# Attention stream of a six-block kernel: the output steps one to two steps later, the next layernorm two steps later

## The chip, the cores and the metric

One core of one Trainium2 chip. The time is the device time of the program in microseconds; less is better.

## What is computed

x is [4, 256, 256] (1024 tokens of 256). Six blocks are added to it in turn: a mixture of experts block (ffn0), an attention without softmax (attn0), ffn0 again, a second mixture of experts (ffn1), a softmax attention (attn1), and ffn1 again. The change lies in attn1 and in what attn1 prepares for the last ffn1:

```
h = layernorm(x)
c_kv = h @ w_dkv.T;  q = (h @ w_q.T), 16 heads of 16
k = c_kv @ w_uk.T;   v = c_kv @ w_uv.T
scores = q k^T / 4 + alibi (slope 0.0625, causal), softmax
x = x + (attn v) @ w_o.T
x = x + 0.5 * ffn1(layernorm(x))
```

With 4 sequences of 256 tokens and 16 heads there are 64 pairs of sequence and head, called heads 0 to 63 here.

## The kernel before

Each engine runs its own list of instructions, written out by hand, and waits on counting semaphores. In attn1 all five lists share one step counter s, from 0 to 77 (64 heads and SUM = 14 steps to drain). What an engine does at a step, in this order:

- TensorE (attn1, from line 1126): scores(s) for s under 64 (lines 1231 and 1234; an even head has two matmuls, an odd one one); scores_t(s-7), the scores once more in transposed form with the softmax shift in them (L1263, L1265); at s mod 4 = 1 shift_turn, four transposes of the shifts of four heads (L1246); at s = 14, 18, ... 74 pv of the next group of four heads, 16 small matmuls (L1282); then the output steps; then project_v at V_STEPS; then at Z_STEP the eight transposes of the next layernorm's result (L808).
- VectorE (from line 2263): bias_min(s), which adds the bias and takes the row minimum (L2319; three parts for an even head, one for an odd); at s mod 4 = 3 shift_hi and shift_lo (L2335, L2340); then its output steps; then at LN_STEPS[0] the layernorm statistics of the first half of x (L1768, L1774).
- ScalarE (from line 1638): out_hi; at s mod 4 = 1 shift_out (L1681); probs(s-7), the exponential (L1688); at LN_STEPS[1] normalise (L1387, four instructions); at s mod 4 = 3 out_t, which copies the result of pv to SBUF (L1695); v_out one step after project_v (L1635); z_hi one step after Z_STEP (L1394, two instructions).
- GpSimd: mask(hd) for each head (L711), and before mask(LN_STEPS[0] - TURN + 1) the scale of the layernorm (ln_scale, L650 to L660).
- SyncE: the DMAs that load the stacks of q and k. They have no step of the list.

**The output steps.** The result of a sequence n (0 to 3), tile t (0 or 1) comes from pv transposed. It is turned back (out_back, TensorE, L1297, four transposes), divided by the softmax sum (out_norm, VectorE, L2348 and L2350), turned again (out_turn, TensorE, L1304, two transposes), split in a rounded part (out_hi, ScalarE, L1699) and a remainder (out_lo, VectorE, L2356), projected with w_o (out_project, TensorE, L793 to L795, six matmuls), and added to x (out_add, VectorE, L2364). OUT_STEPS are TensorE's steps of (back, turn, project) for t = 0 and then for t = 1, counted from 16 n, for n = 0 to 2. VectorE and ScalarE do their part at the step after the one that they follow. n = 3 is done after the loop, in the list of the last ffn1, from out_back on.

All output steps of a sequence, and project_v for n = 2 and 3, use PSUM bank 7. So they wait for each other:

```
def out_back(n, t):                      # TensorE, L1288
    pe.wait_ge(ot_s, 4 * (n + 1))        # out_t of the four groups
    if t == 0 and n < 2:
        pe.wait_ge(v_s, 3 + n)           # v_out
    ...
    elif 2 * n + t:
        pe.wait_ge(yt_s, 2 * n + t)      # the out_add before
```

project_v(3) waits for yt_s of out_add (0,1); out_turn waits for out_norm, out_project for out_hi and out_lo. scores_t(hd) waits for probs(hd-2), and scores of an odd head hd for bias_min(hd-2), of an even head for bias_min(hd-4). The statistics of the next layernorm wait for out_add (1,1); its transposes wait for normalise and for all 64 bias_min; z_hi waits for them. SyncE's list, the weights and all shapes are the same in both kernels.

Of the kernel before, what the change touches and what calls it, by code (L numbers as in the profile page):

```python
# [61 lines left out]
GROUP = 4  # L62
TURN = 7
SUM = 14
OUT_STEPS = (28, 30, 33, 35, 37, 39)
V_STEPS = (25, 41)
LN_STEPS = (57, 61)
Z_STEP = 66
HALF = PAIRS // 2
SLOTS = 16  # L70
STACKED = 16 * 9
# [10 lines left out]
def program(nc, x_in, w0, w1, wr, pre, posts, att0, r0, ident_in, cap_in, iota_in, wa, rows_in, bias_in, split_out, z_rows, y_rows,  # L82
            out,
            stages=STAGES):
    with ExitStack() as ctx:
# [540 lines left out]
        def _(pool):  # L626
# [11 lines left out]
            def ln_scale(p):  # L638
                if p >= norms:
                    return  # L640
                kind = stages[NORMS[p][0]]

                if kind == "ffn0":
                    mul, add = 1.0 + RMS_EPS, RMS_EPS * LN_EPS
                else:
                    mul, add = 1.0, LN_EPS
                pool.wait_ge(mv_s, p + 1)
                if p:
                    pool.wait_ge(zs_s, p)
                nc.gpsimd.tensor_scalar(zs_e[:, :], mv[:, :, 1], mul, add, ALU.mult, ALU.add).then_inc(zse_s, 1)  # L650
                pool.wait_ge(zse_s, p + 1)
                if p:
                    pool.wait_ge(z_s, p)
                if p >= BY_ACT:
                    nc.gpsimd.tensor_scalar(mean_n[:, :], mv[:, :, 0], -1.0, None, ALU.mult).then_inc(mean_n_s, 1)
                nc.gpsimd.tensor_tensor(zs[:, :], zs_e[:, :], half[:, :], ALU.pow).then_inc(zs_s, 1)
                if p >= BY_ACT:
                    pool.wait_ge(mean_n_s, p - BY_ACT + 1)
                    pool.wait_ge(zs_s, p + 1)
                    nc.gpsimd.tensor_tensor(shift_z[:, :], mean_n[:, :], zs[:, :], ALU.mult).then_inc(shift_z_s, 1)  # L660
# [92 lines left out]
            for st in plan:  # L753
                for b in range(2):
# [19 lines left out]
                    elif b == 0:  # L774
                        ln_scale(st.p + 1)
                        for hd in range(4 * HEADS):
                            if hd == LN_STEPS[0] - TURN + 1:
                                ln_scale(st.p + 2)
# [12 lines left out]
        def _(pe):  # L791
# [334 lines left out]
            def attn1(st):  # L1126
# [16 lines left out]
                for s in range(4 * HEADS + SUM):  # L1143
# [15 lines left out]
                    for n in range(3):  # L1159
                        if s - HEADS * n in OUT_STEPS:  # L1160
                            i = OUT_STEPS.index(s - HEADS * n)
                            (out_back, out_turn, out_project)[i % 3](n, i // 3)
                    if s in V_STEPS:
                        project_v(2 + V_STEPS.index(s))
                    if s == Z_STEP and st.after:
                        pe.wait_ge(sm_s, 4 * HEADS)
# [34 lines left out]
            def project_v(n):  # L1201
                if n == 1:
                    pe.wait_ge(qh_s, 1)
                    pe.wait_ge(ql_s, 1)
                elif n == 2:
                    pe.wait_ge(qh_s, 4)
                    pe.wait_ge(ql_s, 4)
                elif n == 3:
                    pe.wait_ge(yt_s, 2)
                for i in range(2):  # L1210
                    t = 2 * (n % 2) + i
                    mm = split3(ps[:, v_bank(n), i * D:(i + 1) * D], ch[:, t * P:(t + 1) * P],
                                cl[:, t * P:(t + 1) * P], wa_h[:, W_V:W_V + D], wa_l[:, W_V:W_V + D], True, True)
                mm.then_inc(v_ps, 1)
# [152 lines left out]
        def _(act):  # L1367
# [14 lines left out]
            def normalise(p):  # L1382
                b = NORMS[p][1]
                act.wait_ge(shift_z_s, p - BY_ACT + 1)
                act.wait_ge(zt_s, KC * zt_count(last_norm(p)))
                for t in range(BT):
                    a = nc.scalar.activation(z2[:, b, t, :], x[:, BT * b + t, :], ACT.Identity, bias=shift_z[:, t:t + 1],  # L1387
                                             scale=zs[:, t:t + 1])
                a.then_inc(z_s, 1)

            def z_hi(p):
                for kc in range(KC):
                    act.wait_ge(zt_s, KC * (zt_count(p) - 1) + kc + 1)
                    nc.scalar.activation(zh[:, kc, :], ps[:, kc, :], ACT.Copy).then_inc(zh_s, 1)  # L1394
# [234 lines left out]
            def v_out(n):  # L1629
                act.wait_ge(v_ps, n + 1)  # L1630
                act.wait_ge(wal_s, WL + 2)
                if n >= 2:
                    act.wait_ge(pv_ps, 4 * (n - 1))
                t = 2 * (n % 2)
                nc.scalar.activation(va[:, t:t + 2, :, 0:HD], ps[:, v_bank(n), :].rearrange("p (t h d) -> p t h d", t=2, d=HD),  # L1635
                                     ACT.Copy).then_inc(v_s, 1)

            def attn1(st):
# [16 lines left out]
                for s in range(4 * HEADS + SUM):  # L1655
                    for n in range(3):
                        for t in range(2):
                            if s - HEADS * n == OUT_STEPS[3 * t + 1] + 1:
                                out_hi(n, t)
                    if s % GROUP == 1 and GROUP < s < 4 * HEADS + GROUP:  # L1660
                        shift_out(s // GROUP - 1)
                    if TURN <= s < 4 * HEADS + TURN:
                        probs(s - TURN)
                    if s == LN_STEPS[1]:
                        normalise(p + 2)
                    if s > SUM and (s - SUM) % GROUP == 1:
                        out_t((s - SUM) // GROUP)
                    if s - 1 in V_STEPS:
                        v_out(2 + V_STEPS.index(s - 1))
                    if s == Z_STEP + 1 and st.after:  # L1670
                        z_hi(p + 2)
# [12 lines left out]
            def probs(hd):  # L1684
                act.wait_ge(t_ps, hd + 1)
                if hd >= 8:
                    act.wait_ge(pv_ps, hd // GROUP - 1)
                nc.scalar.activation(pbt[:, hd // GROUP % 2, hd % GROUP, :], ps[:, turned_bank(hd), 0:3 * P], ACT.Exp,  # L1688
                                     scale=-1.0).then_inc(exp_s, 1)

            def out_t(g):
                act.wait_ge(pv_ps, g + 1)
                if g >= 8:
                    act.wait_ge(ob_ps, 2 * (g // 4 - 1))
                nc.scalar.activation(ot[g // 4 % 2][:, g % 4, :], ps[:, PV_BANK, g % 2 * SEQ:(g % 2 + 1) * SEQ], ACT.Copy).then_inc(ot_s, 1)  # L1695

            def out_hi(n, t):
                act.wait_ge(o2_ps, 2 * n + t + 1)
                nc.scalar.activation(oth[n][:, t, :, :].rearrange("p c q -> p (c q)"), ps[:, out_bank(n, t), 0:D], ACT.Copy)\  # L1699
                  .then_inc(oth_s, 1)  # L1700
# [24 lines left out]
        def _(dve):  # L1725
# [314 lines left out]
            def prepare(p, part):  # L2040

                if p < norms and not (part and p >= BY_ACT):
                    (normalise if part else ln_stats)(p)
# [219 lines left out]
            def attn1(st):  # L2263
# [14 lines left out]
                for s in range(4 * HEADS + SUM):  # L2278
# [11 lines left out]
                    for n in range(3):  # L2290
                        for t in range(2):
                            if s - HEADS * n == OUT_STEPS[3 * t] + 1:
                                out_norm(n, t)
                            if s - HEADS * n == OUT_STEPS[3 * t + 1] + 1:
                                out_lo(n, t)
                            if s - HEADS * n == OUT_STEPS[3 * t + 2] + 1:
                                out_add(p, n, t)
                    if s in LN_STEPS:
                        prepare(p + 2, LN_STEPS.index(s))
                if st.after != "ffn1":  # L2300
# [41 lines left out]
            def out_norm(n, t):  # L2342
                c = 2 * n + t + 1
                dve.wait_ge(ob_ps, c)
                if c > 2:
                    dve.wait_ge(o2_ps, c - 2)
                o = ps[:, out_bank(n, t), :].rearrange("p (h s) -> p h s", s=SLOT)
                V.reciprocal(rec[:, t, :], o[:, :, HD]).then_inc(rec_s, 1)  # L2348
                dve.wait_ge(rec_s, c)
                V.tensor_tensor(on[:, t, :].rearrange("p (h d) -> p h d", d=HD), o[:, :, 0:HD],  # L2350
                                rec[:, t, :].rearrange("p (h o) -> p h o", o=1).broadcast_to([P, HEADS, HD]),
                                ALU.mult).then_inc(on_s, 1)

            def out_lo(n, t):
                dve.wait_ge(oth_s, 2 * n + t + 1)
                V.tensor_tensor(otl[n][:, t, :, :].rearrange("p c q -> p (c q)"), ps[:, out_bank(n, t), 0:D],  # L2356
                                oth[n][:, t, :, :].rearrange("p c q -> p (c q)").bitcast(F32), ALU.subtract)\
                 .then_inc(otl_s, 1)

            def out_add(p, n, t):  # L2360
                c = 2 * n + t + 1
                dve.wait_ge(y_ps, c)
                xt = x[:, 2 * n + t, :]
                V.tensor_tensor(xt, xt, ps[:, out_bank(n, t), 0:D], ALU.add).then_inc(yt_s, 1)  # L2364
                if t == 1 and n % 2:
                    dve.wait_ge(yt_s, c)
                    V.memset(mark[:, :], 0.0).then_inc(x_s[n // 2], 1)
# [95 lines left out]
```

## Time and profile before

| what | us |
|---|---|
| median of 3 runs (504.77 to 506.13) | 505.74 |
| the profiled execution's own time | 502.75 |
| its span in the profile | 500.8 |
| TensorE matmuls busy in it | 459.9 |
| VectorE busy | 363.4 |
| ScalarE busy | 270.7 |
| GpSimd busy | 155.9 |

The profile is of one execution of the program. Times in rows are microseconds from the span's start. A matmul is pipelined, so its printed duration overlaps the next one; the distance between two starts is what a matmul takes of the engine. A bracket behind a row of the timeline is the time that the engine was idle before it, and the instruction that released it. PE is TensorE, PEld its weight loads, DVE VectorE, ACT ScalarE, POOL GpSimd. "PEclk" is the granted TensorE clock as a share of 2.4 GHz.

### The profile page before, as it was taken

The numbers are of one execution on the slowest core, as the hardware profiler recorded it, in microseconds if no ns is written. First come the engines' busy times: TensorE is split into PE (matmuls) and PEld (weight loads), VectorE is DVE, ScalarE is ACT, GpSimd is POOL, SyncE is SP. The second block draws the span as 40 slices with busy tenths as digits, with TensorE's granted clock in tenths as the row PEclk, the third lists the DMA queues.
The fourth block names the chain that finished last, engine by engine and source line by source line (L and its number), as shares of the span: only waits on it lengthen the run. The fifth ranks groups of instructions, "written<-read, shape, count | busy, mean of one in ns | idle before, by whom it ended". The sixth has DMA issues, their size and how long they took to land. (4 is left out here: it accounts for less than half of the span.)

```text
span 500.8 us, 9620 instructions
## 1 busy us (share of the span) xinstructions
PE 459.9 (92%) x3062; PEld 394.1 (79%) x3062; DVE 363.4 (73%) x1196; ACT 270.7 (54%) x599; POOL 155.9 (31%) x221
## 2 busy tenths in 40 slices
PE   1999999999999999999999887999689998799996
PEld 1788888899888898887988766888568777678885
DVE  4668798768456887367885488898398878359685
ACT  3657643455544855445755486364547666644531
POOL 2001000341007710046410436358014334325352
PEclk9999999999999999999999999999899999899999
DMA  6333350033223342142434312671777220000101
GB/s 204 113 93 95 92 193 1 33 116 99 82 88 103 106 131 81 50 146 80 138 89 136 116 41 96 73 112 27 260 202 247 72 65 1 1 2 2 42 1 42
DMA packets 35328, 45.96 MB, mean 92 GB/s; under 512 B 4401, under 2 KB 27825, under 8 KB 35281
## 3 DMA queue, kind: packets, MB, share of 16 engines
q1 hardware_dynamic: 31920, 38.55, 27.0%
q0 software_dynamic: 2304, 6.29, 4.0%
q10 hardware_dynamic: 1056, 0.52, 0.4%
q8 instruction: 26, 0.43, 0.4%
q14 instruction: 22, 0.17, 0.1%
HBM read 26.47 MB, written 16.25 MB: 85 GB/s over the span
## 5 line engine op out<-in xcount | busy, mean ns | idle before, releaser
L793 PE MATMUL ps<-zh,w0u_h 128*128 128x512 f32 x160 | 65.2, 407 | 1.8 <-ACT zh L1394 1.5
L794 PE MATMUL ps<-zh,w0u_l 128*128 128x512 f32 x160 | 63.4, 396 | 0.0
L795 PE MATMUL ps<-zl,w0u_h 128*128 128x512 f32 x160 | 63.3, 396 | 0.0
L2236 DVE SCALAR_TENSOR_TENSOR x<-ps,aff,x 128x256 f32<-128x256 f32 x128 | 53.0, 476 | 10.0 <-PE ps L795 8.3
L793 PE MATMUL ps<-w0d_h,ah 128*128 128x256 f32 (+1 forms) x205 | 58.1, 284 | 0.4 <-DVE al L1902 0.2
L795 PE MATMUL ps<-w0d_l,ah 128*128 128x256 f32 (+1 forms) x205 | 57.2, 279 | 0.0
L794 PE MATMUL ps<-w0d_h,al 128*128 128x256 f32 (+1 forms) x205 | 57.1, 279 | 0.0
L697 POOL TENSOR_TENSOR al<-act,ah 128x512 fp32r<-128x512 f32 x27 | 35.0, 1295 | 45.5 <-ACT ah L1558 43.9
L2319 DVE CUSTOM_DVE_ANT_0 ps<-ps,bias 128x256 f32<-128x256 f32 (+1 forms) x128 | 42.4, 384 | 7.5 <-PE ps L1234 6.6
L711 POOL TENSOR_SCALAR_AFFINE_SELECT pbt<-pbt 128x256 f32<-128x256 f32 x64 | 25.9, 409 | 59.9 <-ACT pbt L1688 59.5
L1423 ACT ACTIVATE gel<-ps 128x512 f32<-128x512 f32 x40 | 23.9, 598 | 36.1 <-PE ps L795 36.0
L793 PEld LDWEIGHTS ps<-w0d_h,ah 128*128 128x128 f32 x205 | 38.5, 188 | 3.1 <-issue 2.0
L723 POOL DMA_INDIRECT z_rows<-z,slots_u x24 | 25.6, 1066 | 44.9 <-DVE slots_u L1956 38.5
L794 PEld LDWEIGHTS ps<-w0d_h,al 128*128 128x128 f32 x205 | 38.5, 188 | 1.1
L1890 DVE TENSOR_TENSOR act<-gel,ps 128x512 f32<-128x512 f32 x40 | 27.3, 682 | 16.0 <-ACT gel L1423 16.0
L793 PE MATMUL ps<-w_h,ah 128*128 128x256 f32 x120 | 34.5, 287 | 4.7 <-DVE x L2236 3.1
L795 PEld LDWEIGHTS ps<-w0d_l,ah 128*128 128x128 f32 x205 | 38.5, 188 | 0.0
L650 POOL TENSOR_SCALAR zs_e<-mv 128x4 f32<-128x4 f32 x12 | 2.5, 210 | 114.7 <-DVE mv L1774 114.6
L793 PEld LDWEIGHTS ps<-zh,w0u_h 128*128 128x128 f32 x160 | 30.8, 193 | 8.8 <-ACT zh L1394 1.8
L1688 ACT ACTIVATE pbt<-ps 128x384 f32<-128x384 f32 x64 | 30.6, 493 | 11.1 <-PE ps L1265 10.4
L1557 ACT ACTIVATE act<-ps 128x512 f32<-128x512 f32 x32 | 19.0, 594 | 32.3 <-PE ps L795 30.6
L1435 ACT ACTIVATE ah<-act 128x512 fp32r<-128x512 f32 x40 | 25.1, 628 | 20.8 <-DVE act L1890 20.0
(240 smaller groups left out, 1354.9 us busy)
## 6 DMA issues: line engine op xcount, KB each, us to landing
stage<-in_w_dram SPq DMA_DIRECT2D x16, 384.0 KB, 3.1
stage<-z_rows SPq DMA_DIRECT2D x21, 256.0 KB, 2.9
y_rows<-tmp SPq DMA_DIRECT2D x21, 256.0 KB, 2.1
qs<-split_out SPq DMA_DIRECT2D x24, 128.0 KB, 2.6
ks<-split_out SPq DMA_DIRECT2D x48, 64.0 KB, 2.4
stage<-in_w_dram SPq DMA_DIRECT2D x8, 256.0 KB, 3.0
z_rows<-tmp SPq DMA_DIRECT2D x1, 1920.0 KB, 8.3
ks<-pad SPq DMA_DIRECT2D x6, 256.0 KB, 9.3
```

Source lines behind the costliest of these rows:

```text
L697: nc.gpsimd.tensor_tensor(lo, act32[:, n % 2, :], hi.bitcast(F32), ALU.subtract).then_inc(al1_s, 1)
L711: nc.gpsimd.affine_select(both, both, pattern=[[0, 2], [1, P]], compare_op=ALU.is_ge, fill=0.0, base=0, channel_multiplier=-1).then_inc(ca ...
L723: nc.gpsimd.indirect_dma_start(z_rows, bass.IndirectOffsetOnAxis(ap=slots_u[:, fb % 2, t, r:r + 1], axis=0), z2[:, fb % 2, t, :], None).th ...
L793: pe.matmul(o, lh, rh, start=start, stop=False, **kw)
L794: pe.matmul(o, ll, rh, start=False, stop=False, **kw)
L795: return pe.matmul(o, lh, rl, start=False, stop=stop, **kw)
L1423: nc.scalar.activation(gel[:, n % 2, :], ps[:, 2 * (n % 2), :], ACT.Gelu_apprx_tanh).then_inc(gelu_s, 1)
L1435: nc.scalar.activation(dst, src, ACT.Copy).then_inc(ah_s, 1)
L1688: nc.scalar.activation(pbt[:, hd // GROUP % 2, hd % GROUP, :], ps[:, turned_bank(hd), 0:3 * P], ACT.Exp, scale=-1.0).then_inc(exp_s, 1)
L1890: V.tensor_tensor(act32[:, n % 2, :], gel[:, n % 2, :], ps[:, 2 * (n % 2) + 1, :], ALU.mult)\
L2236: i = V.scalar_tensor_tensor(xt, ps[:, base + t // 2, (t % 2) * D:(t % 2 + 1) * D], aff[:, b, t, e:e + 1], xt, ALU.mult, ALU.add)
L2319: i = V.tensor_tensor_reduce(s, s, bias[:, cols], 1.0, FAR, ALU.add, ALU.min, nmin[:, hd // GROUP % 2, c, j:j + 1])
```

## The change

```diff
-OUT_STEPS = (28, 30, 33, 35, 37, 39)
-V_STEPS = (25, 41)
-LN_STEPS = (57, 61)
-Z_STEP = 66
+OUT_STEPS = (29, 31, 34, 36, 39, 41)
+V_STEPS = (25, 43)
+LN_STEPS = (59, 63)
+Z_STEP = 68
```

Turning back goes from steps 28 and 35 (of each n, plus 16 n) to 29 and 36, the turn from 30 and 37 to 31 and 39, the projection from 33 and 39 to 34 and 41. project_v(3) goes from 41 to 43. On VectorE the statistics go from step 57 to 59, on ScalarE normalise from 61 to 63 and z_hi from 67 to 69, on TensorE the transposes from 66 to 68, and on GpSimd ln_scale from before mask(51) to before mask(53). What is computed stays the same.

## Rows read from the trace of the kernel before

**Rows 1.** The page, first part: busy us (share of the span), instructions.
```profile
PE 459.9 (92%) x3062; PEld 394.1 (79%) x3062; DVE 363.4 (73%) x1196; ACT 270.7 (54%) x599; POOL 155.9 (31%) x221
```

The columns of the next group: length, busy us (instructions) of PE, PEld, DVE, ACT and POOL, PEclk, DMA share, GB/s.

**Rows 2.** Table of stretches: first output period, and after the long stall.
```profile
388.45:407.00 18.55, 16.87 (x167) 13.90 (x166) 15.13 (x83) 12.47 (x30) 6.64 (x17) 1.00 0.33 90
...
431.00:435.00 4.00, 4.00 (x32) 3.18 (x32) 0.42 (x1) 1.57 (x3) 1.22 (x3) 0.60 0.00 0
```

**Rows 3.** Timeline of TensorE, n = 0: start us, us, engine, line, operation, [idle before].
```profile
388.88 0.66 PE L1297 MATMUL ps<-ident,gel 128*128 128x128 f32 x4 [0.43 <-ACT gel L1695]
...
393.29 0.60 PE L1246 MATMUL ps<-ident,macc 128*128 128x128 f32 x4
393.64 0.36 PE L793 MATMUL ps<-wa_h,ah 128*128 128x256 f32 x1
...
394.41 0.29 PE L1231 MATMUL ps<-ks,qs 96*128 96x256 f32 x1
...
394.98 0.86 PE L1282 MATMUL ps<-pbt,va 128*32 128x256 f32 x16
395.76 0.39 PE L1234 MATMUL ps<-ks,qs 96*128 96x256 f32 x1
...
396.26 0.63 PE L1297 MATMUL ps<-ident,gel 128*128 128x128 f32 x4
...
397.57 0.60 PE L1246 MATMUL ps<-ident,macc 128*128 128x128 f32 x4
398.78 0.44 PE L1304 MATMUL ps<-ident,comb 128*128 128x128 f32 x2 [0.61 <-DVE comb L2350]
...
402.51 0.60 PE L1246 MATMUL ps<-ident,macc 128*128 128x128 f32 x4
403.44 0.38 PE L793 MATMUL ps<-wa_h,ch 128*128 128x256 f32 x1 [0.33 <-DVE x L2364]
```

**Rows 4.** Timeline of VectorE over steps 34 to 36.
```profile
394.85 0.30 DVE L2319 CUSTOM_DVE_ANT_0 ps<-ps,bias 128x128 f32<-128x128 f32 x1 [0.23 <-PE ps L1234]
...
395.70 0.42 DVE L2364 TENSOR_TENSOR x<-x,ps 128x256 f32<-128x256 f32 x1
396.19 0.43 DVE L2319 CUSTOM_DVE_ANT_0 ps<-ps,bias 128x256 f32<-128x256 f32 x1
...
396.92 0.17 DVE L2340 TENSOR_TENSOR macc<-nmin,macc 128x8 f32<-128x8 f32 x1
...
398.01 0.25 DVE L2348 RECIPROCAL rec<-ps 128x16 f32<-128x16 f32 x1
398.30 0.42 DVE L2350 TENSOR_TENSOR comb<-ps,rec 128x256 f32<-128x256 f32 x1
```

**Rows 5.** Timeline of all engines around the statistics of the next layernorm.
```profile
422.03 1.40 DVE L1768 BATCH_NORM_STATS2 bn<-x 128x6 f32<-128x256 f32 x4
...
423.76 0.27 DVE L2319 CUSTOM_DVE_ANT_0 ps<-ps,bias 128x128 f32<-128x128 f32 x1
...
425.16 0.39 PE L1234 MATMUL ps<-ks,qs 96*128 96x256 f32 x1 [0.47 <-DVE nmin L2319]
```

**Rows 6.** Timeline of all engines from normalise to the last turning back.
```profile
427.26 2.06 ACT L1387 ACTIVATE z<-x,shift_z,zs 128x256 f32<-128x256 f32 x4
...
429.84 0.30 PE L1263 MATMUL ps<-qs,ks 128*128 128x128 f32 x1 [1.64 <-ACT pbt L1688]
...
436.62 1.09 ACT L1394 ACTIVATE zh<-ps 128x512 fp32r<-128x512 f32 x2
...
438.31 0.44 ACT L1699 ACTIVATE ah<-ps 128x256 fp32r<-128x256 f32 x1
...
438.78 0.42 DVE L2356 TENSOR_TENSOR al<-ps,ah 128x256 fp32r<-128x256 f32 x1 [1.67 <-ACT ah L1699]
...
440.33 0.86 PE L1282 MATMUL ps<-pbt,va 128*32 128x256 f32 x16
...
441.69 1.09 PE L1297 MATMUL ps<-ident,act 128*128 128x128 f32 x8 [0.50 <-ACT act L1695]
```

## The prediction, made before the changed kernel was run

> **What bounds the kernel now.** I read the page's busy shares first: TensorE is busy 92% of the span [rows 1]. An average hides stages, so next came the table of stretches. In the first output period of the stream, 388.45 to 407.00 (the second is alike), TensorE is busy 16.87 of 18.55 us, VectorE 15.13, ScalarE 12.47 [rows 2]. TensorE's order sets the pace there, VectorE is close behind, and what the change can win or lose is the time for which TensorE stands still in front of an output step. The timeline of TensorE shows these places [rows 3], that of VectorE what each of them waits for [rows 4]. The third view is the end of the stream, where VectorE's layernorm statistics and ScalarE's normalisation cut into it [rows 5, 6].
>
> By a rule of the Trainium skill (Perfetto Trace Analysis, section on identifying the most-contended engine), TensorE's headroom is judged by its weight loads and not by matmul time. By it the period is 13.90 of 18.55 us full on TensorE and 15.13 on VectorE, VectorE would be the engine to relieve, the stalls counted below would be worth nothing, and the sum would be no change.
>
> **The change, part by part.** No instruction is added or removed. Steps move by one or two, so the prices are waits. Step kinds alternate by s mod 4: shift_turn sits on 1, the attention product pv on 2, VectorE's two shift casts on 3; an even head costs VectorE 0.85 us (394.85 to 395.70), an odd one about 0.5 [rows 4].
>
> *Removed.* (a) Turning back (n,0) stands right after scores_t of step 28 and starts at 388.88, with 0.43 bracketed as idle on ScalarE's copy out_t [rows 3]. At step 29 shift_turn stands ahead (0.35, 393.29 to 393.64), but scores_t(22) then waits for the exponentials queued on ScalarE, about 0.2 by the same copy. Gain 0.3 for n=0. For n=1 v_out(3) moves to ScalarE's step 44, and turning back (1,0) at 45 waits for it as long as before: 0. (b) The second turn of each n: shift_turn starts 397.57, the turn could go at 397.93 and goes at 398.78: 0.85 lost to VectorE's norm [rows 3, 4]. With three steps between, it is gone: 0.85, twice. (c) project_v(3): 402.51 + 0.36 against 403.44, 0.57 lost to out_add. Two steps instead of one and a half, with a pv in them: gone, once.
>
> *Added.* (d) The turn (n,0) now follows turning back over an even head. VectorE needs 0.44 until it starts on the scores (394.41 to 394.85), 0.85 for them, 0.29 for the reciprocal (398.01 to 398.30), 0.48 from the norm's start to the turn: 2.06. TensorE has 0.57 to pv, 0.78 for it, 0.50 for an odd step (395.76 to 396.26): 1.85. Wait 0.2, twice. (e) Turning back (n,1) needs out_add (n,0), since both use bank 7. Before, add fell on VectorE's step 34, and a pv covered it: turning back started at 396.26 without a bracket [rows 3]. Now project (n,0) stands behind pv at step 34, and add falls on step 35, behind an odd head and both casts: 0.43 to the scores (395.76 to 396.19), 0.73 to the second cast (to 396.92), about 0.1 to add, 0.48 to TensorE: 1.74. TensorE has an odd and an even step without pv, 1.0. Wait 0.7, twice. (f) Project (n,1) moves to step 41, and needs out_lo of VectorE's step 40, an even head: 0.44+0.85+0.48 = 1.77 after the scores of step 40; TensorE has 0.9 for two steps and 0.36 for shift_turn. Wait 0.5, twice.
>
> Period n=0: -0.3-0.85-0.57+0.2+0.7+0.5 = -0.3. Period n=1: -0.85+0.2+0.7+0.5 = +0.55. At step 60 the changed kernel is 0.25 us behind. The bounds of (d) to (f): nothing, if VectorE works ahead of the pace I give it, and their double (2.8 more), if each wait pushes VectorE's next head back.
>
> *Steps 60 to 62.* Before, the statistics (1.73 us on VectorE, 422.03 to 423.76) are issued at step 57 and hold up scores(61), which goes at 425.16 [rows 5], 0.7 late; turning back (2,0) loses about 0.5 by a wait like that of (a). Afterwards the statistics stand behind the casts of step 59, so scores(61) and shift_turn(14) pass ahead of them, and shift_turn covers (a). Gain 1.2; at step 62 the changed kernel leads by 0.9, at about 425.1 on the clock of the trace.
>
> *The tail.* What was late is late later. scores(63) waits for head 61 behind the statistics, until 427.2; the turn (2,0) for its norm behind head 62, until 428.6. normalise, 2.06 us on ScalarE [rows 6], follows probs(56) instead of probs(54): 428.3 to 430.4, then out_t and out_hi, then probs(57) to 431.5, and scores_t(59) waits for that from 429.8 to 431.6. That is 1.8 us, the stall which scores_t(57) has now (bracket 1.64, until 429.84), only two steps on. After the present stall the granted clock is 0.60 over 431 to 435 [rows 2]: 1.2 GHz for most of it, at a cost of at most 4.00 x 0.40 = 1.6 us. I take the same fall after the moved stall. Then pv(13) and project until 434.4, scores_t(60) and (61), the add, turning back (2,1) at 435.05, eight transposes to 436.3, scores_t(62), (63) and pv(14) to 437.7, the turn (2,1), now alone at step 71. ScalarE meanwhile has probs(62), both z_hi (0.95, as from 436.62), probs(63), out_t(14), and only then out_hi (2,1), at 438.8. VectorE starts out_lo 0.47 later (438.31 to 438.78), project (2,1) 0.5 after that, at 439.8, with about 1.85 us in which TensorE has nothing, since pv(15) is queued behind project. pv is 0.8 behind, and the last turning back 1.36 behind pv (440.33 to 441.69): 441.9, where it was 441.69 [rows 6]. The two-step moves are paid back in the tail, for the steps after 70 hold no scores to cover a chain across three engines. If out_hi keeps its old place in effect (it does not wait for z_hi), 1 us less; if the queues ahead of it run late, 1 us more.
>
> GpSimd's scale step moves with the statistics, ahead of mask(53) instead of mask(51); pv(13), which needs the masks, is behind the stall in any case: nothing, and at most its own delay. No DMA issue moves; the stacks are loaded by then, so SP's queue costs nothing.
>
> **Sum.** +0.25-1.2+1.15 (the tail from step 62) = +0.2, and I take +0.3 for the rounding of six waits. The profiled execution is 502.75 us (span 500.8), so 503.05; on the scale of the runs' median, which is 2.99 higher, 505.74+0.3 = 506.0. The block after it is a full TensorE queue, so the 0.3 passes to the end.
>
> **The rivals.**
>
> *A second fall of the clock (slower).* The stall before project (2,1) is new, about 1.85 us, and as long as the one after which the trace shows the fall; now the idle brackets near the end of the stream are short, 0.50 at 441.69 [rows 6]. For it: the size. Against: TensorE works without a long pause from 431.6 until then. Price: a stretch like the present one, 4.00 x 0.40 / 0.50 = 3.2 us at half speed, less what the wait for ScalarE hides, 1.3 to 1.6: 507.5. It decides from an idle stretch of about 1.6 us in front of project (2,1).
>
> *The new waits of (d) to (f) do not come (faster).* VectorE is idle 3.4 us in the first period [rows 2], so it may stand ready when I have it late. Then the periods keep (a) to (c), -1.7 and -0.85, instead of -0.3 and +0.55: 2.8 us less, 503.2. Against it: each chain was laid from the scores that start it, not from VectorE's backlog.
>
> *The first fall of the clock moves off or shrinks (faster).* The stalls around 427 to 431.6 are nearer together than now, which speaks against; if the slow stretch falls on waiting instead of matmuls, 1.2 us come off: 504.8.
>
> *The change does nothing beyond shifting waits.* By the busy shares alone TensorE has the same work, and each stall that goes comes back: 505.7. This is nearly my own forecast by another way.
>
> **How the numbers follow.** A difference under 0.3% (1.5 us) can't be told from none by a measurement of this kernel. My sum, with its own range of 505.0 to 507.0, and the last rival hold 0.55 together. The second fall gets 0.25, since its stall is only 0.2 longer than the one that did it; the missing waits 0.12; the vanished first fall 0.08. Faster by over 1.5 us takes the missing waits and a little of the last: 0.15. Slower takes most of the second fall and the doubled waits: 0.28. Same: 0.57. The range reaches from between the two faster cases to just above the second fall, 504.0 to 508.0.
>
> **What would show each step right or wrong.** Right: no bracket in front of the turns (0,1) and (1,1) nor project_v(3); new ones in front of turning back (0,1) and (1,1) (waiting for x of out_add, 0.4 to 0.7) and project (0,1) and (1,1) (waiting for the low parts, 0.3 to 0.5); scores(61) without a wait; the longest stall in front of scores_t(59), followed by a clock of 0.5 to 0.6; a second stall in front of project (2,1). Wrong: periods shorter than now by a microsecond each; project (2,1) right behind the turn; or a granted clock below 1 after 439.

## The result and the profile after

| | before | changed |
|---|---|---|
| median of 20 runs, us | 505.76 | 507.83 |
| lowest and highest | 504.08, 507.50 | 505.69, 511.14 |
| ratio to before | | 1.0053 (95%: 1.0038 to 1.0067) |
| profiled execution (span) | 502.75 (500.8) | 507.11 (505.2) |

The changed kernel is 0.5% slower: 2.1 us by the medians, 1.9 to 3.4 by the interval. I had forecast 0.3 us and most of the chance on "same". One run of the kernel before, in the second group of experiments below, took 740.1 us at a mean clock of 0.564 and is left out of its ratios.

The two spans are 4.4 us apart, but 2.42 of that lies ahead of the change: the first pv of the stream starts at 375.67 in one and 378.09 in the other, and nothing up to there differs in the code. So from here on I count from the start of the **first pv** to the start of the **last turning back** (n = 3, after the loop). Before, that is 441.69 - 375.67 = 66.02 us; in the changed kernel:

```profile
378.09 0.86 PE L1282 MATMUL ps<-pbt,va 128*32 128x256 f32 x16
...
446.07 1.09 PE L1297 MATMUL ps<-ident,act 128*128 128x128 f32 x8 [0.51 <-ACT act L1695]
```

67.98 us, 1.96 more, and behind it both need 59.1 us to the end. So all of the loss in the trace that the change can have made is in this distance. (The rows above are from the timeline of the changed kernel: start, duration, engine, line, tiles, idle time before it and releaser.)

The output period n = 0 in TensorE's timeline, to be laid beside [rows 3]:

```profile
399.75 0.63 PE L1297 MATMUL ps<-ident,gel 128*128 128x128 f32 x4 [0.71 <-DVE x L2364]
400.57 0.60 PE L1246 MATMUL ps<-ident,macc 128*128 128x128 f32 x4
401.56 0.86 PE L1282 MATMUL ps<-pbt,va 128*32 128x256 f32 x16
402.81 0.38 PE L1304 MATMUL ps<-ident,comb 128*128 128x128 f32 x2
403.95 0.60 PE L1246 MATMUL ps<-ident,macc 128*128 128x128 f32 x4
404.99 0.36 PE L793 MATMUL ps<-wa_h,ah 128*128 128x256 f32 x1 [0.44 <-DVE al L2356]
...
410.10 0.63 PE L1297 MATMUL ps<-ident,act 128*128 128x128 f32 x4 [0.33 <-issue]
```

The waits before the turn (0,1) (0.61) and project_v(3) (0.33) are gone. In their place turning back (0,1) waits 0.71 for out_add, and project (0,1) 0.44 for out_lo. The last row is turning back (1,0), with 0.33 where it had 0.44. VectorE's side of the 0.71, step 35:

```profile
398.37 0.43 DVE L2319 CUSTOM_DVE_ANT_0 ps<-ps,bias 128x256 f32<-128x256 f32 x1 [0.64 <-PE ps L1234]
398.72 0.14 DVE L2319 DVE_READ_ACCUMULATOR2_ANT nmin<- 128x1 f32 x1
398.90 0.17 DVE L2335 CAST macc<-nmin 128x8 fp32r<-128x8 f32 x1
399.10 0.17 DVE L2340 TENSOR_TENSOR macc<-nmin,macc 128x8 f32<-128x8 f32 x1
399.19 0.41 DVE L2364 TENSOR_TENSOR x<-x,ps 128x256 f32<-128x256 f32 x1
```

VectorE stands idle for 0.64 us although the projection is nearly through: its next instruction is the bias of head 35, whose scores TensorE issues only behind the projection. The add follows that bias and both casts. By this reading it is the order of VectorE's list that makes the wait, not its load; e9 tests it.

The tail, to be laid beside [rows 5, 6]:

```profile
429.76 0.39 PE L1234 MATMUL ps<-ks,qs 96*128 96x256 f32 x1 [0.47 <-DVE nmin L2319]
...
430.80 2.07 ACT L1387 ACTIVATE z<-x,shift_z,zs 128x256 f32<-128x256 f32 x4
...
431.21 0.44 PE L1304 MATMUL ps<-ident,comb 128*128 128x128 f32 x2 [0.83 <-DVE comb L2350]
...
433.92 0.45 PE L1263 MATMUL ps<-qs,ks 128*128 128x128 f32 x1 [1.16 <-ACT pbt L1688]
...
441.23 1.08 ACT L1394 ACTIVATE zh<-ps 128x512 fp32r<-128x512 f32 x2
...
442.82 0.43 ACT L1699 ACTIVATE ah<-ps 128x256 fp32r<-128x256 f32 x1
443.28 0.42 DVE L2356 TENSOR_TENSOR al<-ps,ah 128x256 fp32r<-128x256 f32 x1 [3.12 <-ACT ah L1699]
...
443.85 0.36 PE L793 MATMUL ps<-wa_h,ah 128*128 128x256 f32 x1 [1.66 <-DVE al L2356]
444.71 0.86 PE L1282 MATMUL ps<-pbt,va 128*32 128x256 f32 x16
```

Three waits within 5 us (0.47, 0.83, 1.16), the last behind normalise, and a fourth of 1.66 before project (2,1). The table of stretches shows what follows the third (columns as ahead of [rows 2]; the last but two is the granted clock):

```profile
427.41:433.00 5.59, 4.04 (x39) 2.84 (x37) 4.50 (x26) 4.05 (x9) 3.07 (x8) 1.00 0.01 3
433.00:439.80 6.80, 5.88 (x35) 4.83 (x36) 1.16 (x4) 3.39 (x9) 2.02 (x5) 0.50 0.00 0
439.80:446.00 6.20, 4.10 (x51) 2.82 (x49) 1.98 (x5) 2.77 (x7) 0.82 (x2) 0.99 0.01 1
```

TensorE runs at 1.2 GHz for 6.8 us. In the kernel before the corresponding stretch is 3.4 us long:

```profile
430.80:434.20 3.40, 3.40 (x21) 2.86 (x24) 0.42 (x1) 1.77 (x4) 0.89 (x4) 0.50 0.00 0
```

### The profile page after: what moved, and what is told of

Same layout as the page of the kernel before. It is cut to its first block and busy times, and to the rows that moved or that the text cites. A ratio compares the mean times of both kernels' runs of the same rounds, so it can differ in the third digit from the quotient of the medians.

```text
span 505.2 us, 9620 instructions
## 1 busy us (share of the span) xinstructions
PE 460.8 (91%) x3062; PEld 394.7 (78%) x3062; DVE 363.2 (72%) x1196; ACT 269.5 (53%) x599; POOL 158.8 (31%) x221
```

## The experiments

Two theories. **A**: the loss is in the tail, and a good part of it is the longer slow stretch. **B**: the loss is the new waits in the two output periods. "Distance" is from the first pv to the last turning back, one profiled execution each. Ratios are against runs of the kernel before on the same chip; these medians were 503.1 (e1 to e4), 503.5 (e5 to e8), 503.3 (e9 to e12) and 507.1 us (e13 to e16), so absolute times are compared within a group only.

| run | distance | slow stretch | ratio to before (95%) |
|---|---|---|---|
| before | 66.02 | 3.4 | 1 |
| changed | 67.98 | 6.8 | 1.0053 (1.0038 to 1.0067) |
| e1 changed, waits filled | 65.74 | none | 0.9992 (0.9970 to 1.0014) |
| e2 before, stall filled | 64.51 | none | 0.9971 (0.9948 to 0.9994) |
| e3 first period only | 66.33 | 3.4 | 1.0006 (0.9977 to 1.0035) |
| e4 tail only | 67.54 | 6.8 | 1.0021 (0.9996 to 1.0045) |
| e5 periods only | 65.10 | none | 0.9992 (0.9966 to 1.0017) |
| e6 last tile as before | 67.33 | 6.8 | 1.0026 (0.9996 to 1.0056) |
| e7 before, normalise spread | 63.46 | none | 0.9965 (0.9931 to 0.9998) |
| e8 changed, normalise spread | 65.73 | 3.4 | 1.0018 (0.9986 to 1.0049) |
| e9 changed, VectorE's order | 65.92 | 3.4 | 1.0005 (0.9979 to 1.0031) |
| e10 before, spread and order | 61.41 | none | 0.9903 (0.9871 to 0.9934) |
| e11 e10 with spread statistics | 62.48 | none | 0.9913 (0.9879 to 0.9947) |
| e12 e11 with out_t first | 64.46 | 6.8 | 0.9973 (0.9950 to 0.9996) |
| e13, e14 changed again | 68.96, 68.94 | 6.8, 6.8 | |
| e15 before again | 65.96 | 3.4 | |
| e16 changed, step 62 filled | 65.81 | none | 0.9995 (0.9957 to 1.0033) |

### Take the slow clock away from both: e1, e2

The edit puts matmuls without a reader at the end of TensorE's step, into a bank that nobody uses at that time:

```diff
+FILL = {62: (6, 2, 15), 65: (10, 6, 64)}      # e1; e2: {63: (12, 2, 15)}
...
+                    if s in FILL:
+                        count, bank, value = FILL[s]
+                        pe.wait_ge({2: sht_s, 6: sm_s}[bank], value)
+                        for _ in range(count):
+                            pe.matmul(ps[:, bank, 0:D], wa_h[:, W_O:W_O + P], wa_h[:, W_O:W_O + D],
+                                      start=True, stop=True)
```

Expected of e1:

> The changed kernel with 16 extra matmuls of 256 columns whose results nobody reads (6 at the end of step 62, 10 at the end of step 65), in the two places where TensorE waits. Theory A (the loss is the slow clock: the moved stall is followed by 6.8 us at 1.2 GHz where the kernel before has 3.4): the granted clock stays at 1.0 from 433 to 440, and the time is 2.5 to 3.5 us below the changed kernel's 507.8, so 504.5 to 505.3. Theory B (the loss is the new waits in front of the moved output steps, the clock being only a by-product): at most 0.5 us come off, 507.3 or more. If the extra matmuls run longer than the waits, both are off by that excess, which the trace would show.

Expected of e2:

> The kernel before with 12 such matmuls at the end of step 63, in its long stall. Theory A: the clock stays at 1.0 from 430 to 435 and 1.0 to 1.5 us come off: 504.3 to 504.8; the difference to the changed kernel with the same treatment is then only 0 to 0.6 us. Theory B: 505.7, and the difference to the treated changed kernel stays at about 2 us.

Measured: no clock below 1.0 in the tail of either. The tail of e1 (377.10 at the first pv), its clock and then the rows that are used below:

```profile
425.00:435.00 10.00, 9.19 (x89) 7.46 (x88) 6.26 (x33) 7.44 (x17) 4.66 (x12) 1.00 0.01 2
435.00:443.00 8.00, 5.69 (x64) 4.24 (x63) 2.95 (x7) 3.94 (x10) 1.62 (x4) 1.00 0.00 1
```
```profile
433.09 0.30 PE L1270 MATMUL ps<-qs,ks 128*128 128x128 f32 x1
...
435.08 0.22 PE L1270 MATMUL ps<-qs,ks 128*128 128x128 f32 x1
...
438.53 0.44 PE L1311 MATMUL ps<-ident,comb 128*128 128x128 f32 x2
...
440.62 0.36 PE L794 MATMUL ps<-wa_h,ah 128*128 128x256 f32 x1 [1.66 <-DVE al L2363]
...
442.84 1.09 PE L1304 MATMUL ps<-ident,act 128*128 128x128 f32 x8 [0.51 <-ACT act L1702]
```

and in e2 (376.78 at the first pv):

```profile
441.29 1.09 PE L1304 MATMUL ps<-ident,act 128*128 128x128 f32 x8 [0.50 <-ACT act L1702]
```

So the slow clock costs 67.98 - 65.74 = 2.24 us in the changed kernel and 66.02 - 64.51 = 1.51 in the one before. The treatment takes 0.6 points off the ratio (1.0053 to 0.9992, 3.1 us of 506), and 1.5 us off the kernel before. Theory A holds for the effect of the clock. But A expected 0 to 0.6 us between the two treated kernels, and it is 65.74 - 64.51 = 1.23. So about 1.2 of the 1.96 us are waits, and 0.7 the longer slow stretch. The filling costs something itself: counted from the first pv, scores_t(59) starts at 55.99 in e1 against 55.83 in the changed kernel, and scores_t(57) at 54.23 in e2 against 54.17 in the kernel before, so the 1.23 is some 0.1 too high.

The two treated kernels also show where the waits are. At the eleventh pv after the first (step 58) e1 is 0.35 behind e2 (46.50 against 46.15), at the twelfth 0.70 ahead (50.32 against 51.02), and from there to the last turning back it takes 15.42 us against 13.49. So 0.35 us is lost in the periods, 1.05 won at steps 58 to 62, and 1.93 lost in the tail.

### Where the waits are: e3 to e6

e3 and e4 make OUT_STEPS a table by n:

```diff
+OUT_STEPS = ((29, 31, 34, 36, 39, 41), (28, 30, 33, 35, 37, 39), (28, 30, 33, 35, 37, 39))   # e3, V 25, 43
+OUT_STEPS = ((28, 30, 33, 35, 37, 39), (28, 30, 33, 35, 37, 39), (29, 31, 34, 36, 39, 41))   # e4, LN 59, 63, Z 68
...
+                        if s - HEADS * n in OUT_STEPS[n]:
```

> The new OUT_STEPS for n = 0 alone and V_STEPS (25, 43); n = 1, n = 2, the layernorm and the transposes as before. Theory A and the prediction's working: the period is worth -0.3 to -0.1 us, the rest is unchanged, 505.5 to 505.8, with one slow stretch of 3.4 us. Theory B: +0.7 us or more, the share of this period in a loss of 2.1 us.

> The new steps for n = 2, the layernorm and the transposes, n = 0 and 1 and V_STEPS as before. Theory A: nearly the whole loss or more, +1.4 to +2.5 us (507.2 to 508.2), with a slow stretch of 6 us or more. Theory B: at most +0.7 us, for the two periods with the new waits are left out.

e3: 66.33, +0.31. A small miss of A, with its reason in the trace: the mixture leaves turning back (1,0) at step 44 beside v_out at 44, and it waits 1.11 instead of 0.43. In the changed kernel it stands at 45 and waits 0.33; there the eighth pv after the first comes at 33.03 us against 33.31 before, so the period n = 0 gains 0.28. e4: 67.54, +1.52, slow for 6.8 us, and the same brackets as the changed kernel from 0.48 on. The tail alone makes 1.52 of the 1.96 us of the trace. Its ratio (1.0021) is on A's side in sign, but its interval reaches from nothing to the changed kernel's.

e5 and e6 are the complement and a partial undoing:

```diff
+OUT_STEPS = ((29, 31, 34, 36, 39, 41), (29, 31, 34, 36, 39, 41), (28, 30, 33, 35, 37, 39))   # e5, LN 58, 61, Z 66
+OUT_STEPS = ((29, 31, 34, 36, 39, 41), (29, 31, 34, 36, 39, 41), (29, 31, 34, 35, 37, 39))   # e6, else as changed
```

> The new steps for n = 0 and 1 and V_STEPS (25, 43), the old ones for n = 2 and the transposes; the statistics one step later than before (58, the earliest that the new out_add (1,1) allows), normalise at 61. From the first pv to the last turning back the kernel before takes 66.02 us, the changed one 67.98. Theory A (the loss is in the tail: the slow stretch and the stall before project (2,1)): 66.0 to 66.8, with one slow stretch of 3.4 us and no stall before project (2,1); the time is -0.1 to +0.8 us against the kernel before. Theory B (the new waits in the periods): 67.0 or more, +1.0 us or more.

> The changed kernel, but the second tile of n = 2 is turned back, turned and projected at steps 67, 69 and 71 as before instead of 68, 71 and 73. Theory A1 (the stall of 1.66 us before project (2,1), with its turn alone at step 71, is the main part of the loss): 65.9 to 66.6 from the first pv to the last turning back instead of 67.98, and the slow stretch still 6 us or more. Theory A2 (the slow stretch alone is the loss, a shorter stall only lets the wait for ScalarE come out elsewhere): 67.4 or more.

e5: 65.10, and a surprise: the same stall as before without any fall of the clock in this execution.

```profile
432.43 0.30 PE L1265 MATMUL ps<-qs,ks 128*128 128x128 f32 x1 [1.64 <-ACT pbt L1690]
```

Against e2, which also has no fall, it is +0.59. Of this 0.38 is there at the eleventh pv (46.53 against 46.15), the cost of the periods; most of the rest comes with scores(61), which waits 0.63 for the statistics at step 58, and not at all in the changed kernel. B's 67.0 is refuted. But the execution without a fall is not the rule for e5, as the mean clocks below show. e6: 67.33, slow for 6.8 us. The stall before project (2,1) shrank from 1.66 to 1.14 only, since out_hi still stands behind z_hi and probs(62) on ScalarE. So A1 was wrong by 0.7 us, and the time lies just under A2's 67.4: this stall is not got rid of by TensorE's steps alone.

### One long stall or four short ones: e7, e8

```diff
-                    if s == LN_STEPS[1]:
-                        normalise(p + 2)
+                    if LN_STEPS[1] <= s < LN_STEPS[1] + BT:
+                        normalise(p + 2, (s - LN_STEPS[1],))
```

> The kernel before, with the four instructions of normalise spread over ScalarE's steps 61 to 64, one each, instead of all at 61. Theory A (one long stall lets the clock fall; short ones don't): no clock below 1.0 after 428, 64.3 to 65.3 from the first pv to the last turning back instead of 66.02, 0.7 to 1.7 us faster than before. Theory B (ScalarE's work is what is waited for, however it is cut): 65.8 to 66.2 and the same time.

> The changed kernel with normalise spread over ScalarE's steps 63 to 66. Theory A: the slow stretch of 6.8 us goes or is halved, 65.7 to 66.9 instead of 67.98, with the stall before project (2,1) still there. Theory B: 67.6 or more.

e7: 63.46, no slow stretch, 2.56 us less than before, more than expected: 1.5 is the clock (e2) and 1.05 the stall itself: brackets of 1.64 and 0.18 became 0.18 and 0.67. ScalarE's work is unchanged, so theory B of this pair is refuted. e8: 65.73, 2.25 less than the changed kernel, with half the slow stretch and the 1.66 before project (2,1) untouched. The stall of 1.16 before scores_t(59) is gone from it, and the clock falls all the same, behind the two brackets that are left, 0.47 and 0.84:

```profile
429.00:432.30 3.30, 3.30 (x26) 2.23 (x25) 0.00 (x0) 2.54 (x6) 0.91 (x3) 0.50 0.00 0
```

### VectorE's order: e9 to e12

```diff
                 for s in range(4 * HEADS + SUM):
+                    for n in range(3):
+                        for t in range(2):
+                            if s - HEADS * n == OUT_STEPS[3 * t] + 1:
+                                out_norm(n, t)
+                            if s - HEADS * n == OUT_STEPS[3 * t + 2] + 1:
+                                out_add(p, n, t)
                     if s < 4 * HEADS:
                         bias_min(s)
...
-                            if s - HEADS * n == OUT_STEPS[3 * t] + 1:
-                                out_norm(n, t)
...
-                            if s - HEADS * n == OUT_STEPS[3 * t + 2] + 1:
-                                out_add(p, n, t)
```

> The changed kernel, with out_norm and out_add ahead of bias_min in VectorE's step instead of behind it. If the waits in front of turning back (n,1) (0.71 in the brackets) and of the turns (n,0) are VectorE's order, they go: the twelfth pv after the first starts 1.3 to 1.9 us earlier than now (48.4 to 49.0 us after the first instead of 50.34), the wait in front of project (n,1) (0.44) stays, and the last turning back comes at 66.0 to 66.8 instead of 67.98. If they come from TensorE's own queue or from PSUM, they stay and nothing moves by more than 0.3 us. The slow stretch and the stall before project (2,1) stay in either case.

> The kernel before with normalise spread over four steps and out_norm and out_add ahead of bias_min. If the waits before the turns (n,1) (0.85 start to start), project_v(3) (0.57) are VectorE's order, another 1.7 to 2.3 us come off the spread version: 61.2 to 61.8 us from the first pv to the last turning back instead of 63.46. Against the kernel before that is 3 to 4.5 us. If VectorE's total work is the limit there, it stays at 63.2 to 63.6.

e9: the brackets of 0.71 before turning back (0,1) and (1,1) are gone, so they were VectorE's order. The twelfth pv comes at 49.29 instead of 50.34, 0.3 later than the range I gave, because project (n,1) now waits 0.60 instead of 0.44, and shift_turn(14) 0.59, where the turn (2,0) had waited. Distance 65.92, 0.1 less than the range: of the 2.06 us gained about 1.05 are these waits; the slow stretch, which I had expected to stay, is 3.4 instead of 6.8.

e10, the same order in the kernel before with normalise spread, is the fastest version: 61.41, 4.6 us less than before, ratio 0.9903. Its first output period, from the same distance behind the first pv as in [rows 2]:

```profile
387.71:406.26 18.55, 17.55 (x176) 14.99 (x177) 16.38 (x90) 12.74 (x30) 7.32 (x18) 1.00 0.31 88
```
```profile
388.12 0.66 PE L1297 MATMUL ps<-ident,gel 128*128 128x128 f32 x4 [0.43 <-ACT gel L1697]
...
399.52 0.35 PE L793 MATMUL ps<-wa_h,ah 128*128 128x256 f32 x1 [0.16 <-DVE al L2360]
...
405.14 0.66 PE L1297 MATMUL ps<-ident,act 128*128 128x128 f32 x4 [0.44 <-ACT act L1697]
```

In 18.55 us TensorE is busy 17.55 instead of 16.87 [rows 2], with 176 matmuls instead of 167, and the eighth pv after the first comes 1.25 earlier (32.06 against 33.31). The waits before the turn (0.61) and project_v(3) (0.33) are gone without moving any step of TensorE.

e11 spreads the statistics too, e12 also puts out_t ahead of probs:

```diff
+                    if LN_STEPS[0] <= s < LN_STEPS[0] + BT:          # e11, VectorE
+                        ln_stats(p + 2, (s - LN_STEPS[0],))
...
-                            if hd == LN_STEPS[0] - TURN + 1:         # e11, GpSimd
+                            if hd == LN_STEPS[0] - TURN + 2:
...
+                    if s > SUM and (s - SUM) % GROUP == 1:           # e12, ScalarE, ahead of probs
+                        out_t((s - SUM) // GROUP)
```

> The same, and the layernorm statistics spread over VectorE's steps 57 to 60, one tile each, with GpSimd's scale one mask later (before mask(52)). If the statistics in one piece are what holds up scores(61) (0.7 start to start), 0.4 to 0.7 us more come off; if the work of the statistics itself is what is waited for, nothing does, and normalise may start later by as much as GpSimd's scale does (up to 0.5 us worse).

> The same, and ScalarE's copy out_t ahead of probs in its step. If turning back (n,0) waits for that copy only because probs stands ahead of it (0.38 to 0.43 in the brackets), these brackets go: 0.6 to 1.2 us less over three sequences. If scores_t then waits for probs instead, it is a draw, within 0.3 us.

e11: scores(61) no longer waits, and the twelfth pv comes 0.54 earlier (48.34 against 48.88), as expected. But the stall behind ScalarE is back with 1.43, and the distance is 1.07 longer than in e10, twice the loss allowed for. e12: the brackets before turning back (n,0) go as expected (twelfth pv at 47.53), and then waits of 0.59, 1.43 and 0.65 follow each other, the clock is low for 6.8 us, and 1.98 us of the gain of e11 are lost again: 64.46. Both get TensorE to the tail sooner, where it has nothing but a longer wait. The ratios of e10 and e11 can't be told apart.

### How firm the length of the slow stretch is: e13 to e16

> The changed kernel once more, for the clock after 430 us. If the length of the slow stretch belongs to the kernel (stalls of 0.47, 0.83 and 1.16 us within 5 us): 6 to 7 us again, and 67.7 to 68.2 us from the first pv to the last turning back. If it is the luck of one execution: 3.4 us or none in at least one of the two further looks, and 65.7 to 67.2 us there.

> As the look before it: 6 to 7 us at 1.2 GHz and 67.7 to 68.2 us if the length belongs to the kernel; 3.4 us or none and 65.7 to 67.2 us if it is luck.

> The kernel before once more. If the length belongs to the kernel: 3.4 us and 65.9 to 66.2 us from the first pv to the last turning back. If it is luck: any of 0, 3.4 or 6.8 us, and 64.5, 66.0 or more than 67.

The tail of e13 and its slow stretch:

```profile
436.10:442.90 6.80, 6.61 (x39) 5.56 (x40) 1.23 (x4) 2.65 (x7) 2.01 (x5) 0.51 0.00 0
```
```profile
446.48 0.36 PE L793 MATMUL ps<-wa_h,ah 128*128 128x256 f32 x1 [1.66 <-DVE al L2356]
448.72 1.09 PE L1297 MATMUL ps<-ident,act 128*128 128x128 f32 x8 [0.50 <-ACT act L1695]
```

All three profiled executions of the changed kernel have 6.8 us, both of the kernel before 3.4. So the length belongs to the kernel in these executions. The distances of e13 and e14 are 1 us longer than 67.98, for another reason: there the clock was low once more, at the beginning of the stream,

```profile
368.00:380.00 12.00, 10.55 (x56) 8.80 (x58) 10.50 (x59) 6.16 (x12) 2.42 (x6) 0.77 0.80 233
```

which also reaches over the first pv (from the second pv on they need 64.87 and 64.86 us, the first execution 64.59). Five of the 20 timed runs of the changed kernel have the same mean clock over the span as e13 and e14 (0.983 instead of 0.989) and take 509.2 to 511.1 us, all of the slowest. The kernel before has such runs as often: of its 101 runs that were taken with the experiments, 24 have a mean clock of 0.984 or 0.985, and these are the slower ones of each group by 1.9 to 3.0 us in the median.

The mean clock over the span tells how typical a profiled execution is. In the profiled executions it is 0.994 to 0.997 without a slow stretch in the tail, 0.991 with 3.4 us, and 0.989 or 0.990 with 6.8 us. Of the 20 runs of the changed kernel none is above 0.990; of the 101 of the kernel before 69 are at 0.991 or 0.992 and one above. At 0.993 or more are 10 of 12 runs of e1, 10 of 12 of e2, 6 of 10 of e16, 5 of 10 of e7 and 5 of 6 of e10, but only 4 of 10 of e5: there the stall of 1.64 leaves the clock alone in some executions and not in others. In e9 only two of ten runs are above 0.990, so its profiled execution, with 3.4 us and 0.991, need not be typical. To read lengths of the slow stretch out of mean clocks is an inference; what they show directly is that the treated kernels e1, e2 and e16 have the higher clock in most of their runs.

e16 is e1 with only the fill of step 62 (`FILL = {62: (6, 2, 15)}`):

> The changed kernel with only the 6 extra matmuls at the end of step 62, so that the wait before the turn (2,0) (0.83) is filled and the stall before scores_t(59) (1.16) stays. If two stalls close together make the stretch long: 3.4 us or none, 65.7 to 66.8 us from the first pv to the last turning back, and 1 to 2 us less than the changed kernel. If the last stall alone does it: 6 to 7 us and 67.7 or more.

```profile
433.46 0.30 PE L1270 MATMUL ps<-qs,ks 128*128 128x128 f32 x1 [1.34 <-ACT pbt L1695]
```
```profile
425.00:443.00 18.00, 13.93 (x141) 10.70 (x140) 9.10 (x42) 11.18 (x27) 6.33 (x17) 1.00 0.01 1
```

The last stall stays, even longer (1.34), and the clock does not fall at all. The six matmuls did not fill the wait that I had meant: they stand where scores(63) had waited 0.47, this bracket is gone, and the turn (2,0) still waits 0.66 instead of 0.83. So the last stall alone did not bring the clock down for 6.8 us, the waits ahead of it took part; e8, where the last stall is gone and the clock still falls for 3.4 us, says the same. How the waits add up to a length is not shown.

## Why the prediction was wrong

- **(a) to (f), the periods: right in kind, the waits of (e) and (f) somewhat small.** Forecast for n = 0: -0.3; measured at the eighth pv after the first: 33.03 against 33.31, -0.28. Forecast at step 60: 0.25 us behind; measured at the eleventh pv (step 58): 46.52 against 46.09, 0.43 behind. The new brackets stand where they were forecast, 0.71 and 0.44, and the old ones are gone. Start to start, as the forecast counts, these two waits are 0.87 for 0.7 and 0.68 for 0.5, and the turn (0,0) loses 0.24 for 0.2, without a bracket. The turn (0,1) and project_v(3) come at once.
- **Steps 60 to 62: right in kind.** A lead of 0.9 was forecast, 0.61 measured at the twelfth pv (50.34 against 50.95). scores(61) has no wait; the brackets of 0.47 and 0.83 are at scores(63) and the turn (2,0).
- **The moved stall: right in place and time, not in length.** On the clock of the old trace scores_t(59) was forecast at 431.6; it is at 433.92 - 2.42 = 431.50. But the bracket is 1.16, not the 1.8 of the forecast, since 0.83 is waited before the turn (2,0). The longest stall of the tail is the one before project (2,1), against the sign that I had given.
- **The failing step: "I take the same fall after the moved stall."** The chain prices this fall too low. From the start of scores_t(59) to the end of pv(14) it takes 6.1 us (431.6 to 437.7). In e1, at full speed, the same work takes 433.09 to 438.53 = 5.44; in the changed kernel 433.92 to 441.75 = 7.83. So the chain charged 0.66 for the fall, and it cost 2.39 there. The charge was 0.81 up to the end of the projection (2.8 against 1.99) and nothing behind it; measured are 1.59 more than e1 up to there (437.50) and 0.80 behind it, for the clock is low until 439.8 and not only until the projection is through.

```profile
433.92 0.45 PE L1263 MATMUL ps<-qs,ks 128*128 128x128 f32 x1 [1.16 <-ACT pbt L1688]
...
437.50 0.31 PE L1263 MATMUL ps<-qs,ks 128*128 128x128 f32 x1
...
441.75 0.44 PE L1304 MATMUL ps<-ident,comb 128*128 128x128 f32 x2
```

  Two things are in this. The fall of 3.4 us costs 1.51 us in the kernel before (e2), so even "the same fall" should have been charged 0.85 more; and it is 6.8 us long, which costs 0.73 more still (2.24 against 1.51). By their sum, 1.6, everything behind is late: the turn behind pv(14) was forecast at 437.7 and starts at 441.75 - 2.42 = 439.33; the last turning back was forecast at 441.9 and comes at 446.07 - 2.42 = 443.65. The waits alone the chain had right: 441.9 - 375.67 - 0.66 = 65.57 us from the first pv, and e1 takes 65.74. Its sum of +0.2 was a loss of 1.1 in waits, hidden by a fall that was charged less than the one of the kernel before. In the rivals I saw that the stalls are "nearer together than now", and concluded from it only that the fall would not vanish, not that it could last longer.
- **Project (2,1): right.** A stall of about 1.85 us was forecast, 1.66 stands in the bracket. Between the last two pv there are 3.75 us against 1.70 before, +2.05; forecast was the same two microseconds. It is the largest wait that the change adds, and eats the lead won before it: without slow clocks (e1 against e2) the changed kernel leads by 0.81 at pv(14) (60.64 against 61.45) and is 1.23 behind at the end.
- **The rivals.** The second fall of the clock did not come: behind the first the clock is back at 1.0 in all three profiled executions, with the stall of 1.66 in each. The slower side was entered by the first fall becoming longer, which I had not among the cases. That this rival's 507.5 lies near the median is luck: it adds a second fall that is not there to a first that was charged too little. The missing waits did not come either, though e9 and e10 show that they could be had, by VectorE's order. The rule of the Trainium skill (Perfetto Trace Analysis, section on identifying the most-contended engine) gave no change. By it VectorE is the engine to relieve. The trace doesn't agree: the change cost 1.96 us, and e10, which against e7 changed only when VectorE does its work and not how much, took 2.05 us off TensorE's waits.
- **The size.** Forecast +0.3, trace +1.96, medians +2.07. The range, 504.0 to 508.0, held the median, but only by the rival that did not come; its likely part did not, and a difference of 0.5% had too small a chance.

Open: the ratio of the 20 runs (1.0053, 2.7 us) is somewhat above the 1.96 of the trace, though its interval, from 1.9 us, holds it. Without the five runs with a lower mean clock the mean of the changed kernel's runs is 1.94 above that of the kernel before. For the 20 runs of the kernel before no clocks are on record; in its later runs such a clock is as frequent as in the changed kernel. Open too is by what rule the waits set the length of the fall, and why the stall of 1.64 us is followed by none in some executions of e5.

## What to carry to other kernels

Moving a step later in a schedule by hand moves its wait to the next user of the same bank: look at what the consumer on the other engine does first in its step, and put the short operation that others wait for ahead of the long one that is not ready (this was worth 2.05 us from e7 to e10; the move of steps lost about 1.1 us, the clock apart). In the drain of a pipeline, where no independent work is left, a step moved later can be paid in full, as project (2,1) was here (2.05 us between the last two pv). When a slow stretch of the clock is carried over to a new place in a forecast, charge it what it costs where it is now, and give its length a range. A long operation on a helper engine (normalise, 2.06 us in one piece) was best cut up over steps, also because a wait of TensorE can cost more in clock than in waiting (1.5 us against 1.05, e2 and e7).

## What the runs showed of the hardware

- The slow stretch at 1.2 GHz had only two lengths in the tail, 3.4 us (before twice, e3, e8, e9) and 6.8 us (changed three times, e4, e6, e12), and there was none in the other seven. I had expected one length.
- The same bracket of 1.64 us was followed by a fall in both profiled executions of the kernel before and in e3, and by none in e5. The changed kernel and e16 differ by six matmuls ahead of scores(63), which leave the stall before scores_t(59) in place (1.16 and 1.34), and by 6.8 us of slow clock.
- Waits of 0.47 and 0.84 us with no longer one behind them were followed by 3.4 us at 1.2 GHz in e8.
- The slow clock cost 1.51 us per 3.4 us stretch and 2.24 per 6.8, each from one pair of profiled executions: less than half of it. In the stretch of 6.8 TensorE is busy 5.88 us only, and its first 0.9 us are the end of the wait before scores_t(59).
